# A first stage that turns x and y on VectorE instead of TensorE

## The chip, the cores and the metric

The kernel runs on one core of a Trainium2 chip. Its time is the device time of one execution in microseconds. PE is TensorE, with its weight loads shown apart as PEld; DVE is VectorE, ACT is ScalarE, POOL is GpSimd, and SP is SyncE, which issues the plain DMAs.

## The reference, cut to what matters

```python
N, C = 8 * 1024, 512              # tokens, channels
# 1. modulated linear layer: style[b] scales the channels of x, dcoef[b] the outputs
y = clip(einsum('blc,oc->blo', x * style, weight) * dcoef + bias, -256, 256)
# 2. shared expert, hidden width 1024
shared = (silu(y @ sh_gate_w) * (y @ sh_up_w)) @ sh_down_w
# 3. routing: sigmoid scores of 64 experts in 8 groups; the best 4 groups, then 8 experts
topk_idx, w = route(y @ router_w.T, e_bias)
# 4. for each expert its tokens: (silu(y @ gate_w[e]) * (y @ up_w[e])) @ down_w[e], weighted by w
out = x + shared + routed         # gate_w, up_w: 64 x 512 x 256; down_w: 64 x 256 x 512
```

Everything is float32. The kernel splits each operand of a product into a high part and a low remainder and takes three passes for each product.

## The kernel before, in words

There are three parts. A **setup** turns and splits the weights of the linear layer, the router and the shared expert. The **first stage** goes over 16 blocks of 512 tokens; in it every product has its 512 tokens as the moving columns, so x is needed with channels on partitions. The **expert stage** goes over tiles of 128 (token, expert) entries: a tile's rows of y are gathered from DRAM (`y_rows`) by an indirect DMA of POOL into `x_rows`, turned by PE (`turn_x`, L1223), multiplied by the gate and up weights (L1232), the hidden part is turned (L1241) and multiplied by the down weights (L1250), and the result is added to the output by an indirect DMA.

A block of the first stage has eight chunks of the hidden width, c = 0 to 7. PE does for each chunk `gate` (12 matmuls of 512 columns), `up` (12), and `down` of the chunk before (12); after chunk 7 comes `down` of chunk 7. Between these stand the steps of the **next** block, so that they overlap: in chunk 0 the turning of x (`turn_x`, L469, 16 transposes in two groups of 8), in chunks 1 and 2 the four parts of the linear layer (`make_y`, 12 matmuls each), in chunk 3 the turning of y back to rows (`turn_y`, L489, 16 transposes in two groups of 8), in chunk 4 the router's product and the turning of its logits, in chunk 6 the matmuls that rank tokens within an expert.

ACT and DVE split what PE made: `x_high` and `x_low` read the turned x from PSUM, scale it by `cur` (the block's style) and write the high and low parts `cols_h` and `cols_l`; `y_scale`, `y_clip`, `y_high`, `y_low` do so for y; `y_row` of ACT copies the turned-back y into `yrow`, and SP stores it. DVE's `hidden` (L738 and L30) multiplies the gate and up results and takes the low part; between its two instructions ACT makes the high part. DVE also does the routing: `choose` in chunks 4, 5 and 6, `entries` in chunks 7, 0, 1 and 2, and `result` (L746), which adds the shared expert's output to x.

The order of the work on every engine is written out by hand; engines meet in semaphores. `x_low` of parts 2 and 3 stands behind `hidden` of chunk 0 on DVE, and `make_y` of part 0 waits for all four parts. `down` of chunk c waits for `hidden` of chunk c:

```python
def make_y(q, m, first, v):
    ...
    if m == 0:
        pe.wait_ge(dve_xtl, KC * (q + 1))
```

## Time and profile before

| | us |
|---|---|
| runs of the kernel (median 3939.05) | 3933.24, 3939.05, 15044.9 |
| the profiled execution | 3924.35 |
| its span in the trace | 3922.7 |
| PE busy, share of the span | 3834.2 (98%) |
| DVE busy | 1691.2 (43%) |
| ACT busy | 1507.8 (38%) |
| POOL busy | 1921.1 (49%) |

The third run lies far off the others and is not used for anything here. The first stage lasts to about 1390 us, the expert stage from about 1410 us to the end. Busy times of PE are of overlapping records (a matmul of 512 columns is shown with some 390 ns, while the next one starts 227 ns after it), so the distance between starts tells what an instruction costs, not its own length.

### The profile page before, as it was taken

Reading aid. Unit: us, or ns where it says so; the run is one execution under the profiler, and the core shown is the slowest. Engines: PE = TensorE matmul, PEld = TensorE weight load, DVE = VectorE, ACT = ScalarE, POOL = GpSimd, SP = SyncE. Lnnn points to the kernel's source line nnn. Section 1 sums busy time; section 2 is a strip of 40 time slices with the busy share of each in tenths; the row PEclk is TensorE's granted clock in tenths of the full one; section 3 lists DMA queues with packets and bytes.
Section 4 is the critical chain, followed back from the end, with each engine's and each line's share of the span. In section 5 each row is a group of like instructions: output and inputs, shape, how many; then the busy total and the mean of one; then the engine's idle time right before and its main releaser. Section 6 shows DMA issues by size and latency. Waiting matters only on the chain.

```text
span 3922.7 us, 92670 instructions
## 1 busy us (share of the span) xinstructions
PE 3834.2 (98%) x19160; PEld 3179.8 (81%) x19161; DVE 1691.2 (43%) x4076; ACT 1507.8 (38%) x3339; POOL 1921.1 (49%) x1598
## 2 busy tenths in 40 slices
PE   6999999999999969999999999999999999999998
PEld 5888888888888858888888888888888888888886
DVE  4655555555555633333333333333333333333343
ACT  3222222222222224444444444444444444444444
POOL 1353343333343425555555555555555555555554
PEclk7999999999999989999999999999999999999999
DMA  5121121121122136666666676667676666777766
GB/s 183 44 66 44 44 59 51 49 60 44 50 61 44 33 88 113 113 139 120 113 144 115 114 144 113 143 115 145 113 144 113 144 144 113 145 144 145 146 144 128
DMA packets 296940, 409.20 MB, mean 104 GB/s; under 512 B 116137, under 2 KB 151345, under 8 KB 296817
## 3 DMA queue, kind: packets, MB, share of 16 engines
q0 software_dynamic: 135872, 280.60, 38.2%
q1 hardware_dynamic: 160946, 127.03, 12.3%
q8 instruction: 70, 1.15, 0.2%
q14 instruction: 52, 0.43, 0.1%
HBM read 228.29 MB, written 179.19 MB: 104 GB/s over the span
## 4 chain that ended last, share of the span: by engine, by line
PE 62%; issue 1%; DVE 0%; ACT 0%; ACTq 0%; DVEq 0%; SPq 0%; DMA 0%; POOL 0%; POOLq 0%
PE bank L1232 36%; PE bank L1250 18%; PE bank L1223 4%; PE bank L1241 3%; DVE w_dn_l L30 0%; ACTq L1068 0%; SPq L1068 0%; ACT w_dn_h L1320 0%; DVEq L1079 0%; DMA trow<-tile_table 0%; ACT w_gu_h L1320 0%; ACT x_h L1294 0%; DVE turns L1444 0%; DVE w_gu_l L30 0%; ACTq L1320 0%
## 5 line engine op out<-in xcount | busy, mean ns | idle before, releaser
L1185 POOL DMA_INDIRECT out_dram<-o_rows,to_row x532 | 862.0, 1620 | 930.6 <-issue 750.2
L425 POOL DMA_INDIRECT slot_list<-ent,pos x512 | 504.5, 985 | 822.3 <-PE bank L451 377.0
L1398 DVE TENSOR_TENSOR e_hf<-bank,e_sg 128x256 f32<-128x256 f32 x532 | 225.6, 424 | 1554.6 <-ACT e_sg L1300 1162.6
L1232 PE MATMUL bank<-w_gu_h,x_h 128*128 x2128 | 831.5, 391 | 10.1 <-DVE x_l L30 5.1
L1232 PE MATMUL bank<-w_gu_h,x_l 128*128 x2128 | 830.9, 390 | 0.0
L1232 PE MATMUL bank<-w_gu_l,x_h 128*128 x2128 | 828.9, 390 | 0.0
L1169 POOL DMA_INDIRECT x_rows<-y_rows,from_row x536 | 535.5, 999 | 213.3 <-issue 129.2
L1300 ACT ACTIVATE e_sg<-bank 128x256 f32<-128x256 f32 x532 | 204.4, 384 | 833.5 <-PE bank L1232 831.8
L1232 PEld LDWEIGHTS bank<-w_gu_h,x_h 128*128 128x128 f32 x2128 | 399.9, 188 | 102.1 <-issue 18.9
L1232 PEld LDWEIGHTS bank<-w_gu_h,x_l 128*128 128x128 f32 x2128 | 400.1, 188 | 83.5
L1232 PEld LDWEIGHTS bank<-w_gu_l,x_h 128*128 128x128 f32 x2128 | 400.0, 188 | 82.3
L1250 PE MATMUL bank<-w_dn_h,e_h_h 128*128 x1064 | 463.0, 435 | 0.5 <-issue 0.5
L1250 PE MATMUL bank<-w_dn_l,e_h_h 128*128 x1064 | 418.2, 393 | 0.0
L1250 PE MATMUL bank<-w_dn_h,e_h_l 128*128 x1064 | 414.8, 390 | 0.0
L30 DVE TENSOR_TENSOR x_l<-bank,x_h 128x512 fp32r<-128x512 f32 x534 | 368.9, 691 | 28.8
L1315 ACT ACTIVATE o_rows<-bank,lists 128x512 f32<-128x512 f32 x532 | 367.4, 691 | 0.0
L1223 PEld LDWEIGHTS bank<-ident_r,x_rows 128*128 128x128 f32 x2136 | 241.5, 141 | 95.0 <-issue 25.5
L1294 ACT CAST x_h<-bank 128x512 fp32r<-128x512 f32 x534 | 313.5, 587 | 0.0
L1314 ACT COPY to_row<-lists 128x1 int32 (+1 forms) x532 | 102.4, 192 | 519.2 <-PE bank L1250 510.5
L1223 PE MATMUL bank<-ident_r,x_rows 128*128 128x128 f32 x2136 | 246.0, 239 | 25.8 <-DVE turns L1450 24.9
L652 ACT ACTIVATE sg<-bank 128x512 f32<-128x512 f32 x128 | 76.6, 598 | 426.4 <-PE bank L451 426.4
L1250 PEld LDWEIGHTS bank<-w_dn_h,e_h_l 128*128 128x128 f32 x1064 | 200.5, 188 | 44.7
(244 smaller groups left out, 5988.9 us busy)
## 6 DMA issues: line engine op xcount, KB each, us to landing
xin<-in_x_dram SPq DMA_DIRECT2D x16, 1024.0 KB, 5.8
y_rows<-yrow SPq DMA_DIRECT2D x64, 256.0 KB, 3.1
stage_d<-in_x_dram SPq DMA_DIRECT2D x16, 1024.0 KB
out_dram<-stage_d SPq DMA_DIRECT2D x16, 1024.0 KB, 8.4
raw_gu<-in_L_ffn_gate_w_dram SPq DMA_DIRECT2D x29, 512.0 KB
raw_gu<-in_L_ffn_up_w_dram SPq DMA_DIRECT2D x29, 512.0 KB
raw_d<-in_L_ffn_down_w_dram SPq DMA_DIRECT2D x29, 512.0 KB
lists<-slot_list SPq DMA_DIRECT2D x538, 1.0 KB
```

The source lines that it names most:

```text
L30: return nc.vector.tensor_tensor(out, full, high.bitcast(F32), ALU.subtract)
L425: nc.gpsimd.indirect_dma_start(slots, bass.IndirectOffsetOnAxis(ap=pos[v][:, t, k:k + 1], axis=0), ent[v][:, t, k, :], None).then_inc(scat ...
L1169: nc.gpsimd.indirect_dma_start(xg[u][:], None, y_rows, bass.IndirectOffsetOnAxis(ap=from_row[u][:].bitcast(U32), axis=0)).then_inc(x_ld[u] ...
L1185: nc.gpsimd.indirect_dma_start(out, bass.IndirectOffsetOnAxis(ap=to_row[u][:].bitcast(U32), axis=0), og[u][:], None, compute_op=ALU.add).t ...
L1223: last = nc.tensor.transpose(b_x[u % 2][:, k * P:(k + 1) * P].bitcast(F32R), xg[u][:, k * P:(k + 1) * P].bitcast(F32R), ident_r[:])
L1232: last = nc.tensor.matmul(b_gu[u % 2][:], xp[a][:, u % 2, k, :], wgu[b][:, bass.ds(place, 1), k, :].rearrange("p a n -> p (a n)"), start=( ...
L1241: last = nc.tensor.transpose(b_h[u % 2][:, k * P:(k + 1) * P], hf[:, u % 2, k * P:(k + 1) * P], ident[:])
L1250: last = nc.tensor.matmul(b_o[u % 2][:], hp[a][:, u % 2, k, :], wdn[b][:, bass.ds(place, 1), k, :].rearrange("p a n -> p (a n)"), start=(k ...
L1294: nc.scalar.copy(xp[0][:, u % 2, :, :].rearrange("p k t -> p (k t)"), b_x[u % 2][:]).then_inc(act_x, 1)
L1300: nc.scalar.activation(sg[:, u % 2, :], b_gu[u % 2][:, 0:H], ACT.Silu).then_inc(act_gu, 1)
L1315: nc.scalar.activation(og[u][:], b_o[u % 2][:], ACT.Copy, scale=entry(j, 1, 2).bitcast(F32)).then_inc(act_do, 1)
L1398: nc.vector.tensor_tensor(hf[:, u % 2, :], b_gu[u % 2][:, H:2 * H], sg[:, u % 2, :], ALU.mult).then_inc(dve_gu, 1)
```

## The change

The turning of x and y leaves PE. SP loads x in four pieces for a block: piece a holds channels 128a to 128a+127 and goes to partitions 32a to 32a+31, with token 32s+c on partition 32a+c at place s. DVE's transpose turns 32x32 squares: `x_turn` reads every fourth element of `xin` (a step of 16 bytes) and writes `yt`, so that partition p holds channel 4p+k in chunk k. `x_high` and `x_low` then read `yt` in SBUF. The four `x_turn` of the block after the next stand at the end of chunk 6 on DVE, ahead of `hidden` of chunk 7. `y_turn` reads `yt` plainly and writes `yrow` with a step of 16 bytes; two stand in chunk 3 and two in chunk 4, between `hidden` and `logits`. SP stores each tile of y in four pieces. `y_row` of ACT and both turning steps of PE are gone.

Rows in `y_rows` have their channels in the new order. So the expert stage's `turn_x` reads every fourth element of a gathered row, and the setup reads the linear layer's weight and the style weights with the same step. In these PE instructions the data is the operand that is loaded as weights, and the identity is the one that moves.

```diff
+def every_fourth(ap, k):
+
+    return ap[:, k::4]
...
             def _(sp):
                 def load_x(q):
-                    sp.dma_start(xin[:], rows(xf, q)).then_inc(x_ld, 16)
+                    for a in range(QD):
+                        sp.dma_start(xin[a * SQ:(a + 1) * SQ, :, :],
+                                     xf[bass.ds(q * TB, TB), a * P:(a + 1) * P].rearrange("(s c) e -> c s e", c=SQ)
+                                     ).then_inc(x_ld, 16)
...
                     for t in range(TT):
-                        sp.wait_ge(act_yrow, TT * q + t + 1)
-                        sp.dma_start(rows(y_rows, q, t), yrow[:, t % 2, :]).then_inc(y_st[t % 2], 16)
+                        sp.wait_ge(dve_yrow, TT * q + t + 1)
+                        for a in range(QD):
+                            sp.dma_start(y_rows[bass.ds(q * TB + t * P, P), a * P:(a + 1) * P].rearrange("(s c) e -> c s e", c=SQ),
+                                         yrow[a * SQ:(a + 1) * SQ, t % 2, :].rearrange("p (s e) -> p s e", e=P)
+                                         ).then_inc(y_st[t % 2], 16)
...
-                        if prep and c == 0:
-                            turn_x(i + 1, 0, False)
-                            turn_x(i + 1, 1, False)
...
-                        if prep and c == 3:
-                            turn_y(i + 1, 0)
-                            turn_y(i + 1, 1)
...
-                    nc.scalar.activation(cols[v][0][:, k, :], misc[k % 2][:], ACT.Copy, scale=cur[:, k:k + 1]).then_inc(act_xth, 1)
+                    nc.scalar.activation(cols[v][0][:, k, :], yt[:, k, :], ACT.Copy, scale=cur[:, k:k + 1]).then_inc(act_xth, 1)
...
+                def x_turn(q, k):
+                    if k == 0:
+                        dve.wait_ge(x_ld, 16 * QD * (q + 1))
+                        if some(q):
+                            dve.wait_ge(act_yh, KC * q)
+                            dve.wait_ge(dve_yl, KC * q)
+                            dve.wait_ge(dve_yrow, TT * q)
+                    nc.vector.transpose(yt[:, k, :].rearrange("p (s c) -> p s c", c=SQ),
+                                        xin[:, :, k::KC]).then_inc(dve_xt, 1)
+
+                def y_turn(q, t):
+                    dve.wait_ge(dve_y, KC * (q + 1))
+                    if some(TT // 2 * q + t // 2):
+                        dve.wait_ge(y_st[t % 2], 16 * QD * (TT // 2 * q + t // 2))
+                    nc.vector.transpose(yrow[:, t % 2, :].rearrange("p (s r m) -> p m s r", s=QD, m=KC),
+                                        yt[:, :, t * P:(t + 1) * P].rearrange("p m (s c) -> p m s c", c=SQ)).then_inc(dve_yrow, 1)
...
+                        if prep and c in (3, 4):
+                            y_turn(i + 1, 2 * (c - 3))
+                            y_turn(i + 1, 2 * (c - 3) + 1)
                         if prep and c == 4:
                             logits(i + 1)
                         if prep:
                             for _ in range(chosen_at.get(c, 0)):
                                 next(chosen)
+                            if more and c == NCH - 2:
+                                for k in range(KC):
+                                    x_turn(i + 2, k)
...
                     for k in range(KC):
                         last = nc.tensor.transpose(b_x[u % 2][:, k * P:(k + 1) * P].bitcast(F32R),
-                                                   xg[u][:, k * P:(k + 1) * P].bitcast(F32R), ident_r[:])
+                                                   every_fourth(xg[u][:], k).bitcast(F32R), ident_r[:])
                     last.then_inc(pe_x, 1)
```

On PE, in chunks 0 and 1 of a block, before the change (gate of chunk 0 ends, x is turned around `up`, and after gate of chunk 1 comes `make_y`; rows of 12 like matmuls are cut):

```order
L451 MATMUL bank<-cols_h,sh_gate_l 128x512
L458 ISA
L469 MATMUL bank<-ident,xin 128x128 x8
L451 MATMUL bank<-cols_h,sh_up_h 128x512
...
L467 REGISTER_ALU
L469 MATMUL bank<-ident,xin 128x128 x4
...
L469 MATMUL bank<-ident,xin 128x128 x4
L534 REGISTER_ALU
L451 MATMUL bank<-cols_h,sh_gate_h 128x512
...
L451 MATMUL bank<-cols_h,sh_gate_l 128x512
L475 REGISTER_ALU
L451 MATMUL bank<-cols_h,w_h 128x512
```

Sixteen transposes of x stand in this stretch. The same place now; ISA and REGISTER_ALU rows stand for the sequencer's waits and counts:

```order
L467 MATMUL bank<-cols_h,sh_gate_l 128x512
L467 MATMUL bank<-cols_h,sh_up_h 128x512
...
L467 MATMUL bank<-cols_h,sh_up_l 128x512
L532 REGISTER_ALU
L467 MATMUL bank<-cols_h,sh_gate_h 128x512
...
L467 MATMUL bank<-cols_h,sh_gate_l 128x512
L475 ISA
L467 MATMUL bank<-cols_h,w_h 128x512
```

The two groups of eight transposes are gone, so that one `up` and one `gate` alone lie between gate of chunk 0 and `make_y`.

On DVE, at the end of chunk 6 and in chunk 7, before:

```order
L817 TENSOR_SCALAR tok<-tok 128x4
L760 REGISTER_ALU
L736 REGISTER_ALU
L738 TENSOR_TENSOR stage_d<-bank,sg 128x512
L30 TENSOR_TENSOR h_l<-stage_d,h_h 128x512
L832 TENSOR_TENSOR stage_d<-iota_e,i8f 128x512
```

Here `hidden` follows the last step of the routing at once. And now:

```order
L800 TENSOR_SCALAR tok<-tok 128x4
L743 REGISTER_ALU
L679 ISA
L684 STREAM_TRANSPOSE yt<-xin 128x512 x4
L719 REGISTER_ALU
L721 TENSOR_TENSOR stage_d<-bank,sg 128x512
L35 TENSOR_TENSOR h_l<-stage_d,h_h 128x512
L815 TENSOR_TENSOR stage_d<-iota_e,i8f 128x512
```

The four transposes of x came in between the last step of the routing and `hidden` of chunk 7 (`stage_d<-bank,sg` and `h_l`).

On DVE in chunk 4, before:

```order
L738 TENSOR_TENSOR stage_d<-bank,sg 128x512
L30 TENSOR_TENSOR h_l<-stage_d,h_h 128x512
L727 REGISTER_ALU
L730 TENSOR_REDUCE t<-bank 128x256
L766 TENSOR_TENSOR sbi<-sc,e_bias_b 128x256
```

Here the logits follow `hidden` at once. And now:

```order
L721 TENSOR_TENSOR stage_d<-bank,sg 128x512
L35 TENSOR_TENSOR h_l<-stage_d,h_h 128x512
L690 ISA
L691 STREAM_TRANSPOSE yrow<-yt 128x4x128 x2
L713 TENSOR_REDUCE t<-bank 128x256
L749 TENSOR_TENSOR sbi<-sc,e_bias_b 128x256
```

Two transposes of y came in between `hidden` of chunk 4 and the reduction of the logits.

## Rows read from the trace of the kernel before

**Rows 1.** Busy time by stage: each engine busy, count, clock, DMA share, GB/s.

```profile
60.00:1300.00 1240.00, 1231.71 (x5841) 1015.52 (x5840) 706.46 (x1641) 348.97 (x546) 467.77 (x476) 1.00 0.20 51
...
1500.00:3900.00 2400.00, 2394.05 (x12356) 1992.33 (x12354) 866.65 (x2144) 1087.68 (x2658) 1349.18 (x1030) 1.00 0.68 131
```

**Rows 2.** Timeline of PE in chunk 3 of a block: start, length, instruction.

```profile
606.67 0.39 PE L451 MATMUL bank<-cols_h,sh_gate_h 128*128 128x512 f32 x1
...
609.39 1.04 PE L489 MATMUL bank<-ident,yt 128*128 128x128 f32 x8
...
613.04 1.03 PE L489 MATMUL bank<-ident,yt 128*128 128x128 f32 x8
```

**Rows 3.** Timeline of PE in chunks 0 and 1 of a block.

```profile
655.60 0.49 PE L451 MATMUL bank<-cols_h,sh_gate_h 128*128 128x512 f32 x1 [0.60 <-issue]
...
658.47 1.03 PE L469 MATMUL bank<-ident,xin 128*128 128x128 f32 x8
...
662.08 1.04 PE L469 MATMUL bank<-ident,xin 128*128 128x128 f32 x8
...
665.79 0.50 PE L451 MATMUL bank<-cols_h,w_h 128*128 128x512 f32 x1
```

**Rows 4.** Timeline of DVE in chunk 0 of two consecutive blocks.

```profile
659.96 1.41 DVE L713 SCALAR_TENSOR_TENSOR cols_l<-bank,cur,cols_h 128x512 fp32r<-128x512 f32 x2 [1.89 <-ACT cols_h L614]
...
662.35 0.69 DVE L738 TENSOR_TENSOR stage_d<-bank,sg 128x512 f32<-128x512 f32 x1 [0.98 <-PE bank L451]
...
664.34 1.40 DVE L713 SCALAR_TENSOR_TENSOR cols_l<-bank,cur,cols_h 128x512 fp32r<-128x512 f32 x2
...
745.24 0.69 DVE L738 TENSOR_TENSOR stage_d<-bank,sg 128x512 f32<-128x512 f32 x1 [0.40 <-PE bank L451]
```

**Rows 5.** Timeline of DVE from chunk 5 to chunk 7, then of PE.

```profile
632.81 0.69 DVE L738 TENSOR_TENSOR stage_d<-bank,sg 128x512 f32<-128x512 f32 x1 [2.12 <-PE bank L451]
...
646.78 0.17 DVE L817 TENSOR_SCALAR tok<-tok 128x4 int32<-128x4 int32 x1
...
649.66 0.69 DVE L738 TENSOR_TENSOR stage_d<-bank,sg 128x512 f32<-128x512 f32 x1 [2.71 <-PE bank L451]
...
651.04 0.69 DVE L30 TENSOR_TENSOR h_l<-stage_d,h_h 128x512 fp32r<-128x512 f32 x1 [0.69 <-ACT h_h L658]
...
652.11 0.39 PE L451 MATMUL bank<-sh_down_h,h_h 128*128 128x512 f32 x1
```

**Rows 6.** Groups of DVE instructions by line: busy, mean ns, idle before.

```profile
L738 DVE TENSOR_TENSOR stage_d<-bank,sg 128x512 f32<-128x512 f32 x128 | 88.5, 691 | 267.1 <-PE bank L451 263.8 <-DVE mask L800 2.3
...
L730 DVE TENSOR_REDUCE t<-bank 128x256 f32<-128x512 f32 x16 | 10.9, 684 | 8.0 <-PE bank L506 8.0
...
L836 DVE CAST pos<-pf 128x8 uint32<-128x8 f32 x64 | 11.0, 173 | 2.2
...
L1444 DVE SCALAR_TENSOR_TENSOR turns<-turns,trow 1x145 int32<-1x145 int32 x5 | 2.1, 422 | 0.2
...
L1442 DVE COPY turns<-trow 1x145 int32<-1x145 int32 x1 | 0.3, 269 | 0.0
...
L1447 DVE TENSOR_SCALAR turns<-turns 1x145 int32<-1x145 int32 x1 | 0.2, 225 | 0.0
```

**Rows 7.** Timeline of DVE ahead of the first block.

```profile
59.94 2.50 DVE L30 TENSOR_TENSOR cols_l<-yt,cols_h 128x512 fp32r<-128x512 f32 x4 [0.69 <-ACT cols_h L634]
```

**Rows 8.** Timeline of PE in one expert tile.

```profile
2003.34 0.46 PE L1223 MATMUL bank<-ident_r,x_rows 128*128 128x128 f32 x4
...
2003.63 0.41 PE L1241 MATMUL bank<-ident,e_hf 128*128 128x128 f32 x2
...
2007.99 0.46 PE L1223 MATMUL bank<-ident_r,x_rows 128*128 128x128 f32 x4
```

**Rows 9.** Costliest groups of the page, one of them.

```profile
L1223 PE MATMUL bank<-ident_r,x_rows 128*128 128x128 f32 x2136 | 246.0, 239 | 25.8 <-DVE turns L1450 24.9
```

**Rows 10.** DMA issues of the page: count, KB each, median us to landing.

```profile
y_rows<-yrow SPq DMA_DIRECT2D x64, 256.0 KB, 3.1
```

More of the change, by code:

```diff
@@ L205, in _ @@
                     for m in range(KC):
[L206 removed]
+                        last = nc.tensor.transpose(bank[4 + k][:, m * P:(m + 1) * P], every_fourth(w_raw[:, m, :], k), ident[:])
                     last.then_inc(turned, 1)
@@ L454, in products, with make_y @@
                     return last
-                def turn_x(q, k, first):
-                    if k == 0:
-                        pe.wait_ge(x_ld, 16 * (q + 1))
+                def make_y(q, m, first, v):
+                    xt = cols[v]
+                    if m == 0:
+                        pe.wait_ge(dve_xtl, KC * (q + 1))
+                        if not first:
+                            pe.wait_ge(act_lt, q)
+                    elif m == 1:
                         if some(q - 1):
@@ L462, in turn_x @@
                             pe.wait_ge(dve_lg, 1)
-                    elif k == 1:
-                        if not first:
-                            pe.wait_ge(act_lt, q)
-                    else:
-                        pe.wait_ge(dve_xtl, KC * q + k - 1)
-                    for t in range(TT):
-                        last = nc.tensor.transpose(misc[k % 2][:, t * P:(t + 1) * P], xin[:, t, k * P:(k + 1) * P], ident[:])
-                    last.then_inc(pe_tx, 1)
-                def make_y(q, m, first, v):
-                    xt = cols[v]
-                    if m == 0:
-                        pe.wait_ge(dve_xtl, KC * (q + 1))
-                    elif m >= 2:
+                    else:
                         pe.wait_ge(act_y, KC * q + m - 1)
@@ L590, in body @@
                     down(i, NCH - 1)
-                for k in range(KC):
-                    turn_x(0, k, True)
                 for m in range(KC):
                     make_y(0, m, True, 0)
-                for t in range(TT):
-                    turn_y(0, t)
                 route(0, 0)
@@ L690, in _ @@
                 y_high(0, 0)
-                for t in range(TT):
-                    y_row(0, t)
                 logits_out(0)
@@ L1003, in _ @@
                 for k in range(KC):
+                    x_turn(0, k)
+                for k in range(KC):
                     x_low(0, k, 0)
@@ L1007, in _ @@
                 y_low(0, 0)
+                for t in range(TT):
+                    y_turn(0, t)
                 logits(0)
-                body(0, 0, True, 0)
-                body(1, 0, True, 1)
+                for k in range(KC):
+                    x_turn(1, k)
+                body(0, 0, True, True, 0)
+                body(1, 0, True, True, 1)
                 with dve.Fori(1, NBLK // 2 - 1) as g:
-                    body(2 * g, g, True, 0)
-                    body(2 * g + 1, g, True, 1)
-                body(NBLK - 2, NBLK // 2 - 1, True, 0)
-                body(NBLK - 1, NBLK // 2 - 1, False, 1)
+                    body(2 * g, g, True, True, 0)
+                    body(2 * g + 1, g, True, True, 1)
+                body(NBLK - 2, NBLK // 2 - 1, True, False, 0)
+                body(NBLK - 1, NBLK // 2 - 1, False, False, 1)
         dense.close()
```

67 lines of the change are left out of this document (22 added, 45 removed).

## The prediction

> **What bounds the kernel now.** I first read the busy time by stage. PE is busy in 1231.7 of 1240 us in the first stage and in 2394.1 of 2400 us in the expert stage, at a granted clock of 1.00, so 2.4 GHz; DVE has 706 of 1240 and 867 of 2400 us of work [rows 1]. So whatever leaves or joins PE's stream counts in full, and what joins DVE costs nothing until PE waits for it. The timelines of PE and DVE then tell how near that is. In chunk 3 the 12 matmuls of `gate` take 606.67 to 609.39, 2.72 us, 0.2267 us each; 12 `up` matmuls with 8 transposes take 609.39 to 613.04, 3.65 us [rows 2]. In an expert tile (4.65 us, 2003.34 to 2007.99) four transposes of rows take 0.29 us, 0.0725 us each, while 128 columns at the matmul's rate would be 0.2267 / 4 = 0.0567 us [rows 2, 8].
>
> **What leaves PE.** A group of 8 transposes costs 3.65 - 2.72 = 0.93 us in chunk 3 [rows 2] and 658.47 to 662.08 less 2.72 = 0.89 us in chunk 0 [rows 3]. There are four groups in each of 15 blocks that prepare a next one: 15 x 3.64 = **-54.6 us**.
>
> **A wait that takes their place.** In chunk 0 `hidden` starts on DVE at 662.35, 0.27 us after PE's `up` ended (662.08). Behind it stand `x_low` 2 and 3, which end at 664.34 + 1.40 = 665.74, and PE's `make_y` starts at 665.79 [rows 3, 4]. The second group of transposes and `gate` filled exactly this time. Now `up` ends at 655.60 + 2 x 2.72 + 0.05 = 661.09; `hidden` starts at 661.37 (`x_low` 0 and 1 end at 659.96 + 1.41 = 661.37, as before, since they hang on ACT, which waits for `result` and `cur` of DVE); `x_low` ends 3.39 us behind it, at 664.76, and `make_y` can start at 664.81. PE has one `gate` in between and is there at 661.09 + 2.72 = 663.81: it waits 1.0 us. In every second block DVE goes round its loop first, and had only 0.40 us idle ahead of `hidden` (0.98 in the other) [rows 4]. PE's `up` now ends 0.9 us earlier, so there `x_low` 0 and 1 hold `hidden` some 0.5 us beyond it, and the wait is 1.5 us. Eight blocks at 1.0 and seven at 1.5: **+18.5 us**. What is hidden here is nothing: the turning had been the cover.
>
> **What joins DVE.** The trace has no transpose on DVE. The bounds for one of 128 x 512: a plain pass of two sources is 0.691 us, and a reduction that reads PSUM with wide steps takes 0.684 us too; 8 elements take 0.173 us, so the rest is 1.0 ns for each element. But the only instructions that read SBUF with a wide step (`of_turns`, every 28th word) are slower. The two-source one takes 422 ns for 145 elements, (422 - 173) / 145 = 1.7 ns each. The copy takes 269 ns against 225 for a plain one-source instruction of the same length: 0.66 against 0.36 ns each [rows 6]. Both are 1.7 to 1.8 times the plain price. So a transpose takes 0.69 us at the low end and 0.173 + 512 x 1.7 ns = 1.05 us at the high one, and I take 1.05, since its step of 16 bytes is nearer to those rows. Four in a row start 0.60 us apart where one takes 0.69 [rows 7], so 0.09 us less than their length.
>
> The place that matters is chunk 7. The routing ends at 646.78 + 0.17 = 646.95; `hidden` starts at 649.66 and ends at 651.73; PE's last `down` starts at 652.11 [rows 5]. Four transposes end at 646.95 + 3 x 0.96 + 1.05 = 650.88, so `hidden` starts 1.22 us late, of which 0.38 is spare: PE waits 0.84 us in each of 14 blocks, **+12 us**. At 0.69 us each they end at 649.44, and the cost is nothing. `x_turn` also holds up the early `entries` and `result`, but these only follow `hidden`. The two `y_turn` of chunk 3 stand ahead of a `hidden` for which DVE waits the longest. Those of chunk 4 put the logits, ACT's scores and the first part of `choose` back by 2 us; DVE was idle for 2.12 us ahead of `hidden` 5 [rows 5], and between that and its `down` PE has three more steps of 2.72 us, so I cost it at nothing. If this cover were gone, each 0.1 us would be 1.5 us in all. The same holds for the waits on `y_st`: a store landed in 3.1 us (median) [rows 10], and the third `y_turn` stands a chunk behind the first, 8 us. The load of x has most of a block, also when its packets get shorter. ACT loses four copies in a block and was not late. The three further waits of PE on ACT and DVE are met earlier.
>
> Ahead of the first block the 32 transposes of PE go (some -4 us), four `x_turn` join a serial chain, and the loads of x in 512-byte pieces stand ahead of `stage_u` (up to +4 us): **-2 us**, from -5 to +4.
>
> **The expert stage.** Nothing is removed here, but `turn_x` (2136 transposes [rows 9]) loads its data with a step of 16 bytes. No PE row with such a step exists. From below: nothing, if the load keeps its rate; a gain is excluded, since the count and the size stay. From above, rows of DVE: at 1.7 ns for each of 128 columns a load would be 0.218 us in place of 0.0567. I take the ratio of those rows, 1.75: 0.099 us. A load runs beside the matmul before it. The first of the four has a matmul of 512 columns for cover, the others one of 128, so three of four show their excess of 0.0425 us: 2136 x 3/4 x 0.0425 = **+68 us**. With 1.5 to 2 times the plain price it is 45 to 90 us; the high end, 0.161 x 1602, is 258 us.
>
> The Trainium skill speaks against this step too. "SBUF — State Buffer", section "Door 1: The DMA port swizzle", says that SBUF is read in lines of 16 bytes, and that at least two accesses to one line are needed for full speed; every fourth float gives one. The rows of a wide step agree [rows 6], none shows 16 bytes. The same note also names four floats as a step that is free. Read so, nothing is lost, which is the first rival below.
>
> **Sum.** -54.6 + 18.5 + 12 - 2 + 68 = +42 us. The profiled execution took 3924.35 us, 9 and 15 us less than the two usable timed runs; I set the sum on 3936, their middle: **3978 us**, 1.1% slower. Its own range is 3940 to 4015.
>
> **Rivals.** (1) **The step is free on both engines.** Then only -54.6 + 18.5 - 2 = -38 us is left: 3898 us, 1% faster. For it: the reduction reads PSUM with a wide step at full rate [rows 6], and 16 bytes is far less than 112. Against it: that is PSUM, and both SBUF rows are slow. Chance 0.33. (2) **The load isn't covered at all, or is read at a third of the rate and less.** At 0.099 us without any cover, all 2136 loads show; from an excess of 0.05 us on each the expert stage gives 107 us and the sum passes +79 us, 2%: 4020 us and more, up to 4165 at the upper bound. For it: the distance of four transposes, 0.0725, is above 0.0567 already, so the cover isn't complete. Chance 0.16. (3) **DVE becomes the bound at chunk 7.** If a transpose takes 2 us, since each square is filled and drained in turn, four end at 654.7, `hidden` is 5.0 us late, and PE waits 4.6 us x 14 = 65 us: with a free step on PE 3936 - 38 + 65 = 3963 us. It decides from 0.8 us a transpose. Against it is DVE's idle time everywhere else. Chance 0.05.
>
> **How the numbers follow.** My forecast has 0.46. The range takes in the first rival's value with a little below it (3890) and the nearer part of the second (4025); what lies outside is some 0.1 on either side. A change of less than 2% either way, 79 us, is about what a measurement of this kernel can't tell from none. Slower by more: the second rival and a tail of mine, 0.17. Faster by more would need 79 us, and even all the transposes together are 59: 0.02. Within 2%: 0.81.
>
> **What would show it.** In the profile after: four L1223-like transposes 0.12 us apart or more (0.0725 says rival 1), and a tile of 4.78 us; PE idle before `make_y` of part 0, released by DVE's `cols_l`, near 18 us in all; STREAM_TRANSPOSE at 0.69 to 1.05 us; idle of PE before the last `down` of a block, released by `h_l`, near 12 us; the first stage 24 to 38 us shorter. The prediction fails if the load's step costs nothing, or if the load is slower than any cover.

## The result and the profile after

The changed kernel took 3999.73 us (median of 4 runs, 3998.51 to 4001.32), against 3936.14 us before: a ratio of 1.0176, with an interval of 1.015 to 1.0203. The ratio is estimated from the single runs without the one of 15044.9 us, which the median of before still counts, so it isn't the quotient of the two medians (1.016). The forecast was 3978 us, its range 3890 to 4025. The profiled execution of after has a span of 3996.7 us, 74.0 more than before's 3922.7.

Where the 74 us are is read first by stage. The windows of after, with the columns of [rows 1], show a PE that has lost work in the first stage and is still not free there:

```profile
60.00:1300.00 1240.00, 1191.98 (x5395) 973.30 (x5394) 828.97 (x1780) 320.28 (x488) 479.01 (x478) 0.99 0.23 51
1500.00:3900.00 2400.00, 2398.20 (x11975) 2045.92 (x11974) 835.46 (x2070) 1090.93 (x2570) 1304.94 (x999) 1.00 0.66 126
```

PE is busy in 1192 of 1240 us, where it was in 1232 [rows 1]. In the expert stage it does 11975 matmuls in 2400 us in place of 12356 [rows 1]: 3% fewer with no idle time, so something in its stream costs more. The timeline of PE in one expert tile of after says what:

```profile
2003.03 0.63 PE L1218 MATMUL bank<-ident_r,x_rows 128*128 128x128 f32 x4
2003.49 0.41 PE L1236 MATMUL bank<-ident,e_hf 128*128 128x128 f32 x2
...
2007.83 0.63 PE L1218 MATMUL bank<-ident_r,x_rows 128*128 128x128 f32 x4
```

A tile takes 4.80 us (2003.03 to 2007.83) where it took 4.65, and its four transposes of rows 0.46 us where they took 0.29 [rows 8]. Over 534 tiles 0.15 us are 80 us. The page of after gives the length of the loads, 198 ns each; that of before has 141:

```profile
L1218 PEld LDWEIGHTS bank<-ident_r,x_rows 128*128 128x128 f32 x2136 | 363.9, 198 | 64.2 <-issue 25.4
```

The rows of PEld tell which loads show, first before, then after. The first row of each has the start of the first of the four loads, the second that of the hidden part's loads, which are plain in both:

```profile
2003.11 0.54 PEld L1223 LDWEIGHTS bank<-ident_r,x_rows 128*128 128x128 f32 x4
2003.60 0.20 PEld L1241 LDWEIGHTS bank<-ident,e_hf 128*128 128x128 f32 x2
```

```profile
2002.80 0.71 PEld L1218 LDWEIGHTS bank<-ident_r,x_rows 128*128 128x128 f32 x4
2003.46 0.20 PEld L1236 LDWEIGHTS bank<-ident,e_hf 128*128 128x128 f32 x2
```

The first load stands 0.23 us ahead of the first transpose in both (2003.11 and 2003.34, 2002.80 and 2003.03): it is covered by the matmul of 512 columns. The second load starts with the first transpose. From there to the load of the hidden part it is 0.26 us before and 0.43 after, which is three loads, each 0.057 us longer.

In the first stage the table of waits of after, from 60 to 1340 us (total, times, longest), has two waits of PE that before did not have in this size:

```profile
PE bank L467 <- DVE cols_l L696: 19.8, 15, 4.2
PE bank L467 <- DVE h_l L35: 18.6, 14, 1.4
```

The first stands before `make_y` of part 0, the second before a block's last `down`. DVE's groups by line give the price of a transpose, 1.06 us reading with the step and 1.07 us writing with it:

```profile
L691 DVE STREAM_TRANSPOSE yrow<-yt 128x512 f32<-128x512 f32 x64 | 64.0, 1071 | 6.4 <-DMA y_rows<-yrow 6.4
L684 DVE STREAM_TRANSPOSE yt<-xin 128x512 f32<-128x512 f32 x64 | 63.8, 1056 | 5.8 <-DVE tok L800 5.7
```

How long a block takes is read from DVE's copy of `cur`, one for each block. In before those of blocks 1, 2 and 15, and the `result` of block 14 (the last but one of 16), start so:

```profile
71.03 0.16 DVE L709 COPY cur<-styles 128x8 f32<-128x8 f32 x1
...
158.77 0.16 DVE L709 COPY cur<-styles 128x8 f32<-128x8 f32 x1
...
1241.92 0.16 DVE L709 COPY cur<-styles 128x8 f32<-128x8 f32 x1
...
1322.38 2.48 DVE L746 TENSOR_TENSOR stage_d<-bank,stage_d 128x512 f32<-128x512 f32 x4
```

And in after:

```profile
80.89 0.13 DVE L675 COPY cur<-styles 128x8 f32<-128x8 f32 x1
...
172.05 0.16 DVE L675 COPY cur<-styles 128x8 f32<-128x8 f32 x1
...
1239.49 0.16 DVE L675 COPY cur<-styles 128x8 f32<-128x8 f32 x1
...
1317.05 2.48 DVE L729 TENSOR_TENSOR stage_d<-bank,stage_d 128x512 f32<-128x512 f32 x4
```

From 158.77 to 1241.92 are 13 blocks of 83.32 us; after, from 172.05 to 1239.49, of 82.11. So 15.7 us are gained in the steady blocks and 2.9 in the next one (80.46 to 77.56 us), but the second block begins 13.3 us later: 9.9 lie ahead of block 1's `cur`, 3.4 in the first block. The `result` of block 14 comes 5.3 us earlier, and that of block 15 starts 65.6 us behind it in both. With 79.3 us more in what follows that is the 74 us.

The 9.9 us are seen in the timelines ahead of the first block. DVE and POOL in before:

```profile
35.25 3.59 DVE L709 COPY cur<-styles 128x8 f32<-128x8 f32 x1 [0.31 <-PEq L120]
39.66 1.41 DVE L713 SCALAR_TENSOR_TENSOR cols_l<-bank,cur,cols_h 128x512 fp32r<-128x512 f32 x2 [0.82 <-ACT cols_h L614]
42.34 1.60 DVE L713 SCALAR_TENSOR_TENSOR cols_l<-bank,cur,cols_h 128x512 fp32r<-128x512 f32 x2 [1.27 <-ACT cols_h L614]
...
38.89 8.88 POOL L432 TENSOR_TENSOR sh_down_l<-stage_d,sh_down_h 128x4096 fp32r<-128x4096 f32 x1
```

DVE and then POOL in after:

```profile
37.23 3.59 DVE L675 COPY cur<-styles 128x8 f32<-128x8 f32 x1 [0.31 <-PEq L128]
40.73 4.06 DVE L684 STREAM_TRANSPOSE yt<-xin 128x512 f32<-128x512 f32 x4
44.71 7.57 DVE L696 SCALAR_TENSOR_TENSOR cols_l<-yt,cur,cols_h 128x512 fp32r<-128x512 f32 x4
```

```profile
37.19 3.60 POOL L446 CAST sh_down_h<-stage_d 128x4096 fp32r<-128x4096 f32 x1 [3.95 <-POOLq L128]
40.87 8.87 POOL L448 TENSOR_TENSOR sh_down_l<-stage_d,sh_down_h 128x4096 fp32r<-128x4096 f32 x1
```

A copy of 8 elements that elsewhere takes 0.16 us takes 3.59, as long as POOL's cast; but it does so in before as well, so it is no part of the loss. New is what `x_low` does. In before it has one operand in PSUM, and the four take 1.41 and 1.60 us by twos while POOL subtracts (38.89 to 47.77). In after, with both operands in SBUF, the four take 7.57 us: they end at 52.28, and POOL's subtraction ends at 49.74, 2.54 us before. Between the copy and `x_low` the transposes run at their usual 1.0 us. PE's first `make_y` starts at 52.33; before it started at 44.00. Of these 8.3 us, 2.0 come earlier: `stage_u` lands later, behind x's loads, and ACT's cast of it starts at 25.06 in place of 23.08.

### The profile page after: what moved, and what is told of

The parts are those of the page before. It is cut to its first block, busy times and chain, and to the rows that moved or that the text cites. A ratio compares the mean times of both kernels' runs of the same rounds, so it can differ in the third digit from the quotient of the medians.

```text
span 3996.7 us, 92333 instructions
## 1 busy us (share of the span) xinstructions
PE 3863.7 (97%) x18648; PEld 3249.0 (81%) x18649; DVE 1820.1 (46%) x4204; ACT 1521.1 (38%) x3275; POOL 1928.4 (48%) x1598
## 4 chain that ended last, share of the span: by engine, by line
PE 63%; issue 1%; ACTq 0%; ACT 0%; DVE 0%; SPq 0%; DMA 0%; POOL 0%; DVEq 0%; POOLq 0%
PE bank L1227 36%; PE bank L1245 18%; PE bank L1218 6%; PE bank L1236 3%; ACT w_dn_h L1315 0%; DVE w_dn_l L35 0%; SPq L1063 0%; ACTq L1063 0%; ACTq L1315 0%; ACT w_gu_h L1315 0%; DMA trow<-tile_table 0%; ACTq L1074 0%; DVE turns L1439 0%; POOL out_dram L1180 0%; DMA lists<-slot_list 0%
## 5 line engine op out<-in xcount | busy, mean ns | idle before, releaser
L441 POOL DMA_INDIRECT slot_list<-ent,pos x512 | 513.8, 1004 | 805.7 <-PE bank L467 351.8
L1218 PEld LDWEIGHTS bank<-ident_r,x_rows 128*128 128x128 f32 x2136 | 363.9, 198 | 64.2 <-issue 25.4
L1218 PE MATMUL bank<-ident_r,x_rows 128*128 128x128 f32 x2136 | 338.3, 280 | 25.3 <-DVE turns L1445 24.8
L631 ACT CAST h_h<-stage_d 128x512 fp32r<-128x512 f32 x128 | 79.4, 620 | 396.6 <-DVE stage_d L721 396.6
```

What stands on the lines that cost most here:

```text
L441: nc.gpsimd.indirect_dma_start(slots, bass.IndirectOffsetOnAxis(ap=pos[v][:, t, k:k + 1], axis=0), ent[v][:, t, k, :], None).then_inc(scat ...
L1218: last = nc.tensor.transpose(b_x[u % 2][:, k * P:(k + 1) * P].bitcast(F32R), every_fourth(xg[u][:], k).bitcast(F32R), ident_r[:])
```

## The experiments

The ratios are to runs of the kernel before on the same chip. The medians of these were 3969.1 us (the four kernels on the step of the load), 3957.2 (the second trace of before, the two waits of PE, the version with y alone), 3969.2 (the longer loop, the start, the last version) and 3932.4 (the shorter loop); the second set of experiments shows where they differ. The changed kernel itself ran on none of these chips, so a difference to its 3999.7 us is one between chips; the traces stand beside it.

**The step of the load.** Four kernels differ in nothing but the expert stage's load.

```diff
-  xg[u][:, k * P:(k + 1) * P].bitcast(F32R), ident_r[:])     # before
+  xg[u][:, k::4].bitcast(F32R), ident_r[:])                  # step of 4, in the kernel before
+  xg[u][:, k * 64:k * 64 + 255:2].bitcast(F32R), ident_r[:]) # step of 2, in the kernel before
+  xg[u][:, k * 32:k * 32 + 382:3].bitcast(F32R), ident_r[:]) # step of 3, in the kernel before
...
-  every_fourth(xg[u][:], k).bitcast(F32R), ident_r[:])       # changed kernel
+  xg[u][:, k * P:(k + 1) * P].bitcast(F32R), ident_r[:])     # changed kernel, plain load
```

> The kernel before, with one edit: the expert stage's turning of rows loads every fourth element of a gathered row, as the changed kernel does (the rows are stored in plain order here, so channels meet other weight rows and the output is not the reference's; the amount of work is the same). Theory A, the step of the load alone makes the expert stage longer: four transposes take 0.46 us in place of 0.29, a tile 4.80 us in place of 4.65, and the kernel is 80 to 90 us slower than before, near 4020 us. Rival B, the longer tile of the changed kernel comes from something else of it (how y_rows were written, the buffers' places): then this kernel stays within 10 us of before.

> The kernel before, the expert stage's load takes every second element (8 bytes apart) of 255 in a row, four times from other starting points; some channels are read twice and some never, so the output is not the reference's. Theory A1, SBUF is read in lines of 16 bytes and two hits in a line suffice (the Trainium skill, SBUF — State Buffer, section Door 1: The DMA port swizzle): nothing, four transposes in 0.29 us, 3936 us. Rival A2, the price grows with the distance between elements: a third of the way to the step of four, four transposes in 0.34 us, 3960 us. Rival A3, every step above one costs the same: like the step of four, near 4020 us.

> The kernel before, the expert stage's load takes every third element (12 bytes apart); some channels are read twice and some never, so the output is not the reference's. Theory A1, lines of 16 bytes with two hits needed: three of four lines have one hit (of four elements, two share a line), so nearly the price of the step of four: four transposes in 0.42 us, near 4000 us. Rival A2, price by distance: two thirds of the way, 3990 us. Rival A3: like the step of four, near 4020 us.

> The changed kernel, with one part undone: the expert stage's turning of rows loads 128 plain elements again (the rows are stored in the new order, so channels meet other weight rows and the output is not the reference's). Theory A: the tile falls from 4.80 to 4.65 us, the kernel from 3999.7 to near 3917, which is some 15 to 20 us faster than before: the first stage's own gain less what its start-up lost. Rival B: the tile stays at 4.80 and the time near 4000 us.

Measured: step of 4 in the kernel before, 4030.9 us, ratio 1.0165 (1.0131 to 1.02); step of 2, 4044.3 us, 1.0202 (1.0167 to 1.0237); step of 3, 4040.6 us, 1.0187 (1.0148 to 1.0225). The plain load in the changed kernel: 3935.2 us, 0.9923 (0.9893 to 0.9954). PE's timeline with the step of 2, then in the changed kernel with the plain load:

```profile
2003.37 0.62 PE L1223 MATMUL bank<-ident_r,x_rows 128*128 128x128 f32 x4
2003.83 0.40 PE L1241 MATMUL bank<-ident,e_hf 128*128 128x128 f32 x2
2008.19 0.62 PE L1223 MATMUL bank<-ident_r,x_rows 128*128 128x128 f32 x4
```

```profile
2003.76 0.46 PE L1218 MATMUL bank<-ident_r,x_rows 128*128 128x128 f32 x4
2004.06 0.40 PE L1236 MATMUL bank<-ident,e_hf 128*128 128x128 f32 x2
2008.41 0.46 PE L1218 MATMUL bank<-ident_r,x_rows 128*128 128x128 f32 x4
```

Four transposes take 0.46 to 0.47 us with a step of 2, 3 or 4, and 0.29 to 0.30 with none; a tile 4.80 to 4.82 against 4.65. By the medians the step of 4 costs 62 us in the kernel before and the plain load gives back 65 in the changed one, not 80: kernels with the plain load have times in two groups some 15 us apart (see the last section), and the first trace of before is of the faster one. So the expert stage's loss is the step of the load alone, in either kernel. And it is a price for each step above one that was tried, 2, 3 and 4, not one that grows with it. The Trainium skill's rule ("SBUF — State Buffer", section "Door 1: The DMA port swizzle": lines of 16 bytes, two hits in a line for full speed) would have made a step of 2 free, since it hits each line twice; the trace doesn't agree for this load, with 0.46 us against 0.29. (By that rule a step of 3 has one hit in two of three lines, not in three of four as the expectation has it; the reading is the same.) Without the step, the changed kernel is 0.8% faster than before on its chip, and level with the 3936.1 us of the first chip.

**A wait that before has on some chips.** In the three kernels with a step, the first stage, which they leave as it was, ended 32 to 34 us later than in the first trace of before. The kernel before was traced a second time, unchanged.

> The kernel before, unchanged, for a second trace of it. In the three runs that only edit the expert stage's load, the first stage (untouched by the edit) ended 33 us later than in the first trace of before (result of block 15 at 1355 in place of 1322 us), with a wait of 1.6 us before PE's make_y in each block, behind an idle ACT ahead of its last cols_h. Theory C: the kernel before itself has this wait in some executions and on some chips, independent of any edit: then its time here is either near 3925 with no such wait or 3950 to 3970 with it, and the trace says which. Rival D: the edits brought it: then this trace has no idle ACT there and its time is within 5 us of the others on its chip.

It took 3961.1 us, 1.0012 of the others on its chip (0.9992 to 1.0033), and its `result` of block 14 starts at 1349.07. Its table of waits from 60 to 1340 us:

```profile
PE bank L451 <- DVE cols_l L713: 20.2, 9, 3.3
ACT cols_h L614 <- remote: 16.3, 11, 2.2
```

Its ACT in chunk 0 of a block has idle time that no engine or queue in the trace ends:

```profile
504.95 0.69 ACT L614 ACTIVATE cols_h<-bank,cur 128x512 fp32r<-128x512 f32 x1 [2.15 <-remote]
```

So theory C holds: the kernel before has this wait itself, and by the medians of its runs it had it in three of five sets. (In every trace from these three chips ACT also has 54 to 121 us of waiting put down to `issue`, that is to nobody, and there is none in the first traces of before and after and in that of the shorter loop. There, what a table gives to one releaser is a lower bound.) Its times run from 3919 to 3983 us, while those of the changed kernel and of each variant of it with the stepped load (4 to 9 runs each) lie within 9 us of each other. Where before has the wait, the change should cost less than 1.8%: the 3999.7 us of the first chip are 1.1% above 3957.2 and 0.8% above 3969.2. No run shows this on one chip.

**Code that is loaded again.** The same traces differ in one more thing. The view of the DMA queues from 200 to 1200 us (packets, MB, share) has this row in the first trace of before, and this one in after:

```profile
q8 instruction: 54, 0.88, 0.5%
```

```profile
q8 instruction: 5, 0.08, 0.0%
```

Two kernels asked what it hangs on and whether it costs anything.

```diff
# in the changed kernel: PE's turning of the logits, nine times over
-                    for t in range(TT):
+                    for t in 9 * list(range(TT)):
                         last = nc.tensor.transpose(misc[0][:, t * P:(t + 1) * P], lt[:, ...], ident[:])
...
# in the kernel before: a quarter of PE's turning of y
-                    for k in range(KC):
+                    for k in range(1):
                         last = nc.tensor.transpose(misc[(t + 1) % 2][:, k * P:(k + 1) * P], yt[:, k, ...], ident[:])
```

> The changed kernel with 32 more transposes of 128 columns for each block on PE (the logits are turned nine times over, with the same result), so that PE's loop of two blocks has as many instructions as before the change. In the traces of the kernel before, some 53 packets of 16 KB of code came in over queue 8 from 200 to 1200 us; after the change 5. Theory E: PE's loop was too long to stay loaded, and the reloading is what makes ACT idle (cols_h and sg, released by nothing on the core) in four of five traces of before: the packets come back to some 53, ACT's idle time of 35 to 40 us too, and the runs scatter by over 0.5%. Rival F: the packets come back, but ACT has no such idle time and the runs scatter by 0.2% or less: then the reloading costs nothing, and the idle time has another cause. Rival G: the packets stay at 5: then it is not PE's length. Time: 16 blocks of 32 transposes at 0.06 to 0.11 us, so 4030 to 4055 us under F or G and up to 30 us more under E.

> The kernel before with 12 of the 16 transposes of y left out in each block (the output is not the reference's), so that PE's loop is 12 matmuls shorter for each block; ACT's instructions stay as they are. It asks whether PE's code reloading and ACT's idle time ahead of the last cols_h of chunk 0 (in the traces of before on three chips, not in the first) hang together. PE's own work falls by 15 blocks x 12 x 0.11 = 20 us. Theory E: the packets of queue 8 fall from some 53 to under 15, ACT's unexplained idle time goes, and the runs lie within 0.2% of each other, some 50 us under before on the same chip. Rival F: with or without the packets, ACT's idle time stays at 35 to 40 us, and the kernel is some 20 us faster than before on the same chip, with the same scatter.

The longer loop took 4059.3 us (ratio 1.0231, 1.0198 to 1.0265), with 51 packets; the shorter one 3911.7 us (0.9965, 0.9946 to 0.9984), with 4:

```profile
q8 instruction: 51, 0.84, 0.5%
```

```profile
q8 instruction: 4, 0.07, 0.0%
```

So the packets are PE's loop: a few matmuls more or fewer in a block decide whether it stays loaded. But the longer one scattered by 4 us only (4056.9 to 4060.9), and of the idle time that its table calls `remote` ACT had 5 us, none ahead of `cols_h`: the reloading doesn't bring this wait, and here rival F holds.

It isn't free, though. In each trace with 51 or more packets PE stops once in each round of its loop of two blocks, ahead of the first `gate` matmul, for 0.5 to 1.2 us with no releaser in the trace; [rows 3] begins with one such stop, and this is one of the longer loop:

```profile
687.27 0.49 PE L467 MATMUL bank<-cols_h,sh_gate_h 128*128 128x512 f32 x1 [0.89 <-issue]
```

That is six stops and 4.2 us in the first trace of before, 5.4 us in the longer loop, and none in any trace with 4 or 5 packets, that of after among them. That the stop is the reloading is inferred from this: the two go together in all 14 traces.

The shorter loop doesn't settle ACT's wait for the kernel before, because it ran on a chip where before itself took 3932.4 us and so had no such wait to lose. By its trace the `result` of block 14 starts at 1309.03, 13.4 us earlier than in before: part of the 20 us of transposes left out comes back as 8.8 us of waiting for `yrow`, where it was 1.6. What makes ACT idle stays open. No variant of the changed kernel, in which ACT reads the turned x in SBUF and not in PSUM, had this wait ahead of `cols_h`; what stands there under `issue` is at most 1.0 us.

**The two waits of PE.** One kernel moves the two late `x_low`, one makes the transposes of x cheaper.

```diff
# x_high and x_low of all four parts ahead of h_high and hidden in chunk 0 (DVE; ACT likewise)
-                            x_low(i + 1, 0, 1 - v)
-                            x_low(i + 1, 1, 1 - v)
+                            for k in range(KC):
+                                x_low(i + 1, k, 1 - v)
...
-                            x_low(i + 1, 2, 1 - v)
-                            x_low(i + 1, 3, 1 - v)
```

> The changed kernel with all four x_high and x_low of a block ahead of h_high and hidden in chunk 0, on ACT and DVE. Theory A: PE's wait before make_y of part 0 (19.8 us in 15 blocks after the change) comes from x_low 2 and 3 standing behind hidden; it goes, hidden of chunk 0 starts 1.4 us later, and down of chunk 0 has a whole chunk of cover: 15 to 20 us faster than the changed kernel, 3980 to 3985 us where that takes 3999.7. Rival B: hidden of chunk 0, now late, holds up down of chunk 0 or the next gate, and the wait only changes its place: within 5 us of the changed kernel.

```diff
# x_turn reads runs of 32
-                                        xin[:, :, k::KC]).then_inc(dve_xt, 1)
+                                        xin[:, :, k * SQ:(k + 1) * SQ]).then_inc(dve_xt, 1)
```

> The changed kernel, but x_turn reads runs of 32 neighbouring elements in place of every fourth (channels meet other weight rows, the output is not the reference's; the amount of work is the same). Theory A, as in the prediction's price: the step of 16 bytes makes the transpose 1.05 us; plain it takes 0.69 us, hidden of chunk 7 starts 1.4 us earlier, and PE's wait before the last down (18.6 us in 14 blocks) falls to 5 us or less: 13 to 18 us faster than the changed kernel. Rival B: the transposing itself takes 1.05 us whatever the step (y_turn, which reads plainly and writes with the step, took 1.08 too): the times and the wait stay.

The first took 3977.9 us (ratio 1.0061, 1.0041 to 1.0081), the second 3980.6 us (1.0052, 1.003 to 1.0073): 22 and 19 us under the changed kernel. By their traces the `result` of block 14 starts at 1296.8 and 1300.7 in place of 1317.05. PE's waits, first with `x_low` moved, then with the plain read:

```profile
PE bank L467 <- DVE h_l L35: 19.2, 14, 1.7
...
PE bank L467 <- DVE cols_l L693: 1.9, 1, 1.9
```

```profile
PE bank L467 <- DVE cols_l L696: 10.3, 10, 2.5
PE bank L467 <- issue: 8.3, 5, 1.8
...
PE bank L467 <- DVE h_l L35: 0.3, 1, 0.3
```

Each wait goes with its own cause. The plain read leaves the other one whole: the five waits under `issue` stand before `make_y` too, and 10.3 and 8.3 are 18.6 us in 15 blocks, as against 19.8. The rivals fall: the late `hidden` of chunk 0 holds up nothing, and a transpose does get cheaper without the step. Its row in the second kernel:

```profile
L684 DVE STREAM_TRANSPOSE yt<-xin 128x512 f32<-128x512 f32 x64 | 39.8, 679 | 5.8 <-DVE tok L800 5.7
```

0.68 us plain, 1.06 with a step of 16 bytes.

**The start.** POOL's split of the shared down weights waits for the first four `x_low`:

```diff
+                pool.wait_ge(dve_xtl, KC)
                 nc.gpsimd.tensor_copy(sdw[0][:], stage_d[:]).then_inc(pool_split, 1)
```

> The changed kernel; POOL waits for the four x_low ahead of the first block before it splits the shared down weights. Theory A: these four x_low took 7.57 us after the change (1.89 each, 0.71 each elsewhere) because they read both operands in SBUF while POOL splits the weights (3.60 and 8.87 us): without POOL they take 2.9 us, the first make_y starts at 47.7 in place of 52.3 us, and the kernel is 4 to 5 us faster than the changed one; POOL ends at 60 us, long before down of chunk 0 needs the weights. Rival B: something other than POOL slows them, and they stay at 7.57 us. Rival C: the split, now beside DVE's later instructions, takes the same time from them: the first block's cur stays at 80.9 us.

It took 3994.9 us (ratio 1.0067, 1.0047 to 1.0088), 5 us under the changed kernel. DVE, then POOL, ahead of the first block:

```profile
36.70 0.17 DVE L676 COPY cur<-styles 128x8 f32<-128x8 f32 x1 [0.31 <-PEq L128]
...
40.70 2.70 DVE L697 SCALAR_TENSOR_TENSOR cols_l<-yt,cur,cols_h 128x512 fp32r<-128x512 f32 x4
48.70 7.74 DVE L703 TENSOR_SCALAR yt<-yt 128x512 f32<-128x512 f32 x1 [5.31 <-ACT yt L601]
```

```profile
47.15 9.02 POOL L449 TENSOR_TENSOR sh_down_l<-stage_d,sh_down_h 128x4096 fp32r<-128x4096 f32 x1
```

The copy is down to 0.17 us, a gain of 3.4 us that before doesn't have, and the four `x_low` are back to 2.70: theory A is right about the cause. The wait then falls on the next of DVE's instructions, `y_clip`, which takes 7.74 us in place of 0.43, up to 0.3 us after POOL's end (56.17). It costs less there, as PE has the other parts of `make_y` to do: PE starts at 43.45 in place of 52.33, and `cur` of block 1 at 72.19 in place of 80.89, so rival C falls too. Of these 8.7 us, 4.5 are left at the `result` of block 14 (1312.53): the 13 steady blocks took 0.27 us each longer. That isn't the edit, since they took 0.24 us longer in the changed kernel with the plain load too, whose first stage is untouched; the cause stays open.

**Versions without the step.** The first stores y in runs of 32 and puts the gate and up weights into the same order by their DMAs. The second also reads x in runs of 32, moves `x_low` and lets POOL wait, as above.

```diff
-  yrow[:, t % 2, :].rearrange("p (s r m) -> p m s r", s=QD, m=KC)
+  yrow[:, t % 2, :].rearrange("p (s m r) -> p m s r", s=QD, m=KC)
...
+  for a in range(QD):
+      sp.dma_start(raw[0][a * SQ:(a + 1) * SQ, bass.ds(half, 1), :, n * H:(n + 1) * H].rearrange("p a k n -> p (a k) n"),
+                   w[bass.ds(e, 1), a * P:(a + 1) * P].rearrange("e (k j) h -> j (e k) h", j=SQ)).then_inc(raw_gu_ld, 16)
...
# the second one: the linear layer's weights in the order of x, by ACT in the setup
+  nc.scalar.copy(w_ord[:, m, :].rearrange("p (k a j) -> p a k j", a=QD, k=KC),
+                 w_raw[:, m, :].rearrange("p (a k j) -> p a k j", a=QD, k=KC)).then_inc(ordered, 1)
```

> The changed kernel with another order of y's channels: y_turn writes runs of 32, a row of y_rows has channel 128m + 32a + r at place 128a + 32m + r, turn_x of the expert stage loads 128 neighbouring elements, and the gate and up weights are loaded in four pieces each so that their rows stand in the same order. The result is the reference's. Theory A: all of the expert stage's loss is the stepped load: tile 4.65 us, 75 to 85 us faster than the changed kernel, near 3920 us, 0.4% faster than before. Rival B: the weights' smaller DMAs come late or collide with the gathers, and 20 us or more of it are lost again: 3940 us and more. If y_turn's write was slowed by its step, it falls from 1.08 to below 0.8 us; if not, it stays.

> A version that should beat both kernels; its result is the reference's. On top of the variant with y's channels in runs of 32: x_turn reads runs of 32 as well (the linear layer's weights are put into the same channel order, by four copies of ACT in the setup, the style weights by the copies that were there), all four x_high and x_low stand ahead of h_high and hidden in chunk 0, and POOL splits the shared down weights after the first x_low. From the runs so far: 20 us from the order of x_low, 16 us from the plain read, 4 us from POOL, less some 3 us for the copies in the setup: 37 us under the variant (3933.9 us, profiled 3922.8), so 3885 to 3900 us, 1.0 to 1.7% faster than before. Rival: hidden of chunk 0, now late, and the plain read gain at the same wait, so that their gains do not add up: 3905 to 3915 us.

The first took 3933.9 us, ratio 0.9944 (0.9924 to 0.9964): the tile is back at 4.65 us. The smaller DMAs cost 3.5 us, once: SP issues the first gate and up weights in 2.03 and 1.93 us in place of 0.42 and 0.40, and PE waits 28.4 us ahead of the first tile in place of 24.9. The second took 3885.3 us (3871.8 to 3891.8), **ratio 0.9782 (0.9753 to 0.981)**, against before at 3969.2 on that chip; it is also 1.3% under before's 3936.1. Its four transposes of rows take 0.29 us and a tile 4.65 (2002.79 to 2007.44). `y_turn`, now without the step in its write, takes 0.69 us:

```profile
L701 DVE STREAM_TRANSPOSE yrow<-yt 128x512 f32<-128x512 f32 x64 | 41.8, 688 | 9.6 <-DMA y_rows<-yrow 6.6 <-issue 3.0
```

Both of PE's waits are gone from its table of waits but for 0.2 us, and the `result` of block 14 starts at 1268.2, 54 us before the 1322.4 of the kernel before and 50 before the 1318.4 of the version with y alone. The three gains alone were 20.2, 16.3 and 4.5 us in the traces: they add up, with 9 us more that no run separates, and the rival of this run falls.

## Why the prediction was right, step by step

The direction, the likeliest case and the range held; the time was 22 us above the forecast. On the profiled executions +42 us was predicted and +74 measured, so the sum was off by 32; some 10 us of that were made up by setting it on 3936 and not on the profiled 3924.35, which is luck: the profiled run of after lay 1.2 us from the median. One of the signs named, a first stage 24 to 38 us shorter, failed: it ended 5.3 us earlier. The steps:

**What left PE** (-54.6 us) held: both groups are gone, and nothing else took their time on PE. The sum left out that PE's stops at its loop would go with them, 4.2 us.

**The wait before `make_y`** (+18.5 us) measured 19.8 us: 4.2 in the first block alone, 0.86 in nine of the others and 1.5 to 1.8 in five, where 1.0 and 1.5 had been worked out. The mechanism is shown by the kernel that moves `x_low`.

**Chunk 7** (+12 us) measured 18.6 us, 1.33 in each of 14 blocks in place of 0.84. A transpose took 1.06 us where 1.05 was worked out: 1.7 ns for each element, the rate of the rows with a step of 28 words, holds for one of four. What the sum left out is that DVE doesn't start at once, and that the routing itself ends later in some blocks. In two blocks of after:

```profile
570.30 3.98 DVE L684 STREAM_TRANSPOSE yt<-xin 128x512 f32<-128x512 f32 x4 [0.65 <-DVE tok L800]
...
652.84 3.99 DVE L684 STREAM_TRANSPOSE yt<-xin 128x512 f32<-128x512 f32 x4 [0.30 <-DVE tok L800]
```

The idle time ahead of the transposes is 0.65 us in six of the 14 blocks, 0.30 in six and 0.04 in the two outside the loop, 5.8 us in all. In blocks of the first kind the routing ends 5.15 us before PE could begin its last `down`, where before had 5.00; in those of the second kind 4.80, where before had 5.16 (the prediction worked from such a block); in the two outside the loop 4.57, where before had 5.28. So all come to about the same 1.3 us. What makes DVE idle there, and the routing later, no run shows.

**Ahead of the first block** (-2 us, -5 to +4) is the step that failed: it measured +9.9, and the first block lost 3.4 more where a gain was forecast, with the wait of 4.2 us before its `make_y`. The prediction counted the later `stage_u` (2.0 us, within its "up to +4") and four `x_turn` in a serial chain, and gave the chain no price. It has eight: the four of block 1 stand between the logits and `cur` of block 1, whose starts lie 4.46 us apart in place of 0.61. And `x_low` was put at nothing. But the change makes it read both operands in SBUF where one was in PSUM, and POOL works on SBUF at that time: the first `x_low` waited until POOL's instruction had ended, 4.9 us in all. The instructions of [rows 7], with two operands in SBUF as well, run free, but at 59.94 us POOL was done. This is what the Trainium skill has in "SBUF — State Buffer", section "Who interferes with whom": DVE and GpSimd share a port pair under an exclusive lock, and a DVE instruction with two SBUF inputs contends with a GpSimd one that reads SBUF. The trace agrees, 7.57 us against 2.70 when POOL is made to wait, and the transposes with one input ran beside POOL at 1.0 us each. Two inputs aren't the whole condition, though: the copy of `cur` and `y_clip` have one each, and waited 3.59 and 7.74 us. `y_turn` also waits for the stores in the first block, 2.29 and 0.83 us, where the prediction had nothing.

**The expert stage** (+68 us) measured 80 us by the tile, 79.3 by the stage's length in the traces. The assumption that the first of four loads is covered by the matmul of 512 columns before it, and that three show, held: the PEld rows above have it. The price of 0.0425 us for one was too low: 0.46 - 0.29 = 0.17 us over three loads is 0.057 each, which would be 91 us, and 0.02 us a tile come back elsewhere. In between, the 80 us come nearer to the 68 than the price alone would. That a ratio taken from rows of another engine came so near is luck too: by the runs with a step of 2 and 3 the distance doesn't count here, only whether the elements are neighbours.

**The rivals.** The free step falls on both engines. The uncovered load falls as it was put, since the first load is covered; but its limit was an excess of 0.05 us on each of four, 0.2 us a tile, and three of 0.057 come to 0.17, so it was near. (Its upper end of 4165 us counts three loads of four; with all of them, as the rival says, it is some 4250.) DVE as the bound at chunk 7 falls with the price of 1.06 us.

So what was too low is the time ahead of the first block (-2 against +9.9: 12 us), the expert stage (68 against 79.3: 11) and the 15 blocks (24.1 us predicted; 18.6 gained in 14 and 3.4 lost in the first: 9, chunk 7 and the first block above all): together the 32 us between +42 and +74.

## What to carry to other kernels

Work that is moved off the busiest engine takes its layout with it: look at who reads the new order, and how often. Here some 55 us were taken from PE, and every fourth element in a gathered row cost 80 us in 2136 loads; the same squares with runs of 32 and the weights' rows permuted by their DMAs cost 3.5 us once, and took 66 us off the changed kernel by the medians of two chips. With `x_low` moved, x in runs of 32 and POOL made to wait, a kernel 1.8% slower than before became one 1.3% faster than the same 3936.1 us, and 2.2% faster than before on its own chip. And where an operand goes from PSUM to SBUF, check what GpSimd does at that time.

## What the runs showed of the hardware

Weight loads of 128 columns, one behind the other, start 0.143 us apart with a step of 4 floats and 0.086 without, and steps of 2 and 3 cost about as much (four transposes 0.46 to 0.47 us against 0.29); behind a matmul of 512 columns the longer load doesn't show. DVE's transpose of 128 x 512 floats takes 0.68 us plain, and 1.06 whether the step of 16 bytes is in its read or in its write. A DVE copy of 8 elements waited 3.59 us for a GpSimd cast to end, and an instruction of two sources that ran beside GpSimd's subtraction with one of them in PSUM waited for its end with both in SBUF. A loop on PE was loaded again in every round (54 packets of 16 KB in 1000 us), at 0.5 to 1.2 us a round, and 12 matmuls less for each block ended that. In the kernel before, the `result` of block 14 started at 1322 us in one trace and at 1349 in another, and its times go by the chip; the cause stays open. Kernels with the plain load also show times in two groups some 15 us apart (3922 to 3928 and 3940 to 3943 us for the version with y alone). The traces place it in the expert stage: from the `result` of block 14 to the end it is 2600 us in both traces of before and 2604 in the version with y alone (traced at 3924.5 us), but 2614 to 2617 in the changed kernel with the plain load, the shorter loop and the last version. The cause stays open.
